# Moving the issue of the padded-key transfers from SyncE to ScalarE in a fused cross-attention and mixture kernel

## The chip, the cores and the metric

The kernel runs on one core of one Trainium2 chip. The metric is the device time of one execution in microseconds. Engines are named as in the profile: PE is TensorE, DVE VectorE, ACT ScalarE, POOL GpSimd, SP SyncE; a q behind the name is that engine's sequencer, which also issues its DMAs.

## The reference, cut to what matters

Sixteen batches of 128 tokens with 256 channels; 32 heads of 8 channels; a mixture of 32 experts follows the attention.

```python
q = (layernorm(x) @ Wq).reshape(b, n, 32, 8)
k, v = split(ctx @ Wkv, 2)                 # ctx: 16 x 128 x 128
q, k = apply_axial_rope(q, pos), apply_axial_rope(k, pos)
w = softmax(einsum('bqhd,bkhd->bhqk', q, k) / sqrt(8))
x = x + einsum('bhqk,bkhd->bqhd', w, v).reshape(b, n, 256) @ Wout + bout
x = x + mixture(layernorm(x))              # gate, top 6 of 32 experts, shared expert
```

## The kernel before, in words

The attention is a software pipeline over batches. Each engine has its own program, a list of periods (`periods`, line 341): periods -3 to 1 and 12 to 17 are written out, 2 to 11 are a hardware loop of five passes with two periods each, so that every even period from 4 on follows a back edge. In period b the engines work on batches b-2 to b+4 at different stages. A period has eight steps g = 0 to 7, one for each quad (4 heads).

For a batch, TensorE computes logits twice. `logits_q` (line 851) has queries on the partitions: four heads at once, from the stationary `qst` and the moving `kz`. `kz` is the padded form of the keys: [128, 4, 8, 128], in which the 32 rows of head j stand in plane j and all else is zero, so that one matmul of 512 columns keeps four heads apart. VectorE takes the row maxima (`row_max`, line 662), TensorE turns them (`transpose_max`, line 855), VectorE copies them to `mxs` (line 669), and SyncE moves them by a DMA of 2 KB into spare rows of `qst` (line 443), two quads at a time: four "halves" a batch, numbered 0 to 3 by `half`. Then `logits_k` (line 864) computes logits again with keys on the partitions, now less their maxima, ScalarE takes the exponential (line 558), and `weigh_values` (line 875) multiplies with V. In period b, steps 0 to 7 of `logits_k` belong to batch b. `logits_q` runs ahead: quads 5 to 7 of batch b in steps 0 to 2, then quads 0 to 4 of batch b+1 in steps 3 to 7. The first of these (step 3) is the first reader of batch b+1's padded keys, and waits for `kz_in`. Maxima halves 2 and 3 of batch b are sent in steps 1 and 3, halves 0 and 1 of batch b+1 in steps 5 and 7. `logits_k` waits for a half at every even step; at step 4 it is half 2, sent in step 1.

How `kz` is filled: the keys of batch b+1 are turned by TensorE (`transpose_k`, line 834) in step 6 of period b-1 and copied by VectorE to `kT` (`evac_kT`, line 697), which signals `kT_ok`. SyncE then issues four DMAs (line 436), one for each group of 32 partitions, 64 KB each, from `kT` into `kz[m1.par]`. There are two `kz` buffers; this one was last read for batch b-1. In SyncE's program the four stand at the top of period b, behind the maxima's transfer of step 7 of the period before, and wait until all exponentials of batch b-1 are done (`exp_ok`), which also implies that `logits_k` of b-1 has finished. In periods -1 and 0 they wait for `kz_zero` and `kT_ok`. Behind them on SyncE come the maxima half 2 (step 1), the context of batch b+4 (line 448), and maxima halves 3, 0 and 1. VectorE's next `evac_kT` waits until the four transfers have read `kT`.

ScalarE's period b (line 552): step 0 is the exponential of quad 0, the copy of V of batch b+1 (line 563), the copy `xcT` of batch b+3 (line 544) and `evac_OT` of batch b-1 (line 608); step 1 an exponential and the copy of `qst` (line 579); step 2 an exponential and the copy of q and k (line 569), which GpSimd's `rope` waits for; step 4 an exponential and `norm`; step 5 the copy `attnT`. In the loop, it also issues the mixture's weight loads, 352 KB each, behind its work of steps 1, 4 and 6 (`load_first`, lines 131 and 133). They are read only in the mixture, from about 292 us. The exponential of quad 0 needs a free `pw` buffer, that is TensorE's `weigh_values` of quad 4 of batch b-1, which stands behind `project_v` (line 841) in TensorE's step 0. The copy of V waits until `weigh_values` of batch b-1 is through. In TensorE's program `transpose_q` (line 827, step 1) waits for this copy, `project_k` (line 816, step 1) for `xcT`, `project_q` (line 820) follows in step 2.

Nothing of the mixture is touched by the change.

Of the kernel before, what the change touches and what calls it, by code (L numbers as in the profile page):

```python
# [36 lines left out]
QUADS, SLOT = NH // 4, 32  # L37
# [237 lines left out]
def attention(nc, sem, X, identf, st2, ring, ahead, hidden, bank, x, ctx_in, pos, wq, wkv, wout, bout):  # L275
    with ExitStack() as es:
# [16 lines left out]
        kT = sb("kT", [P, QUADS, P], F16)  # L293
        kz = [hidden.kz[:, i] for i in range(2)]
# [27 lines left out]
        consts, consts2, kz_zero = sem("consts"), sem("consts2"), sem("kz_zero")  # L322
# [7 lines left out]
        qstT_mm, kstT_mm, qst_ok, kT_ok = sem("qstT_mm"), sem("kstT_mm"), sem("qst_ok"), sem("kT_ok")  # L330
# [10 lines left out]
        def periods(eng, period):  # L341
# [8 lines left out]
            for n in range(12, NB + 2):  # L350
                period(Batch(n // 2, n % 2))

        def inside(b, lo=0, hi=NB - 1):

            return not isinstance(b.n, int) or lo <= b.n <= hi
# [54 lines left out]
        @block.sync  # L410
        def _(sp):
            sp.dma_start(POS[:, :, :], pos.rearrange("b p a -> p b a")).then_inc(pos_in, 16)
            for c in range(4):
                part = slice(XPART[c], XPART[c + 1])
                sp.dma_start(X[:, part, :], xr[:, part, :]).then_inc(x_in[c], 16)
                if c == 0:
                    sp.dma_start(CT[0][:, :], ctx_in[0]).then_inc(ctx_in_s[0], 16)
                    sp.dma_start(WKV[:, 0:D], wkv[:, 0:D]).then_inc(w_in, 16)
                    sp.dma_start(WQ[:, :, :], wq.rearrange("(c p) n -> p c n", p=P)).then_inc(w_in, 16)
                    sp.dma_start(CT[1][:, :], ctx_in[1]).then_inc(ctx_in_s[1], 16)  # L420
            sp.dma_start(WKV[:, D:], wkv[:, D:]).then_inc(bo_in, 16)
            sp.dma_start(BO[:, :], bout.rearrange("(a n) -> a n", a=1).broadcast_to([P, D])).then_inc(bo_in, 16)
            sp.dma_start(WO[:, :, :], wout.rearrange("(c p) n -> p c n", p=P)).then_inc(bo_in, 16)

            def period(b):
                m1, m4 = b + 1, b + 4
                if inside(m1):


                    if isinstance(b.n, int) and b.n < 1:  # L430
                        sp.wait_ge(kz_zero, 2)
                        sp.wait_ge(kT_ok, m1.n + 1)
                    else:
                        sp.wait_ge(exp_ok, QUADS * b.n)
                    for j in range(4):
                        sp.dma_start(kz[m1.par][32 * j:32 * j + 32, j, :, :],
                                     kT[32 * j:32 * j + 32, :, :]).then_inc(kz_in[m1.par], 16)
                for g in (1, 3, 5, 7):
                    who, half = (b, (g + 3) // 2) if g < 5 else (m1, (g - 5) // 2)
                    if inside(who):  # L440
                        k = 4 * who.n + half
                        sp.wait_ge(mxs_ok, k + 1)
                        sp.dma_start(qst[who.par][MAXROW:P:SLOT, 2 * half:2 * half + 2, :],
                                     mxs[half % 2][:, :]).then_inc(mr_in[half % 2], 16)
                    if g == 1 and inside(m4, 2):
                        at_least(sp, xcT_mm, m4.n - 1)
                        sp.wait_ge(consts, 2)
                        sp.dma_start(CT[m4.par][:, :], ctx_in[m4.n]).then_inc(ctx_in_s[m4.par], 16)
            periods(sp, period)
            hidden.store(sp)  # L450

# [78 lines left out]
        @block.scalar  # L530
        def _(act):
            act.wait_ge(turn_s, 5)
            act.activation(ang[:, :, :, :, :], turns[:, :, :, :, :], ACT.Sin, scale=TWO_PI).then_inc(sin_s, 1)

            def norm(m):
                act.wait_ge(rs1_ok, 8 if not isinstance(m.n, int) or m.n > 9 else 6 if m.n > 3 else 4 if m.n else 2)
                at_least(act, xcT_mm, m.n)
                act.activation(xn[:, :], X[:, m.n, :], ACT.Identity, bias=nb1[:, m.n, :],
                               scale=rs1[:, m.n, :]).then_inc(xn_ok, 1)

            def evac_xcT(m):
                at_least(act, xcT_mm, m.n + 1)
                at_least(act, v_mm, m.n - 1)
                act.copy(xcT[m.par][:, :, :], M1[:, 0:3 * P].rearrange("p (c t) -> p c t", c=3)).then_inc(xcT_ok, 1)

            norm(Batch(0, 0))

            def hi(m):
                act.wait_ge(hT_mm, m + 1)
                act.copy(hidden.hT[m // 8][:, 0, :, m % 8 * P:m % 8 * P + P], HBANK[m % 2][:, 0:D].rearrange("p (c t) -> p c t", c=DK)).then_inc(hT_hi, 1)  # L550

            def period(b):
                m1, m2, m3, m4, o = b + 1, b + 2, b + 3, b + 4, b + -1
                for g in range(QUADS):
                    if inside(b):
                        act.wait_ge(st_mm, QUADS * b.n + g + 1)
                        at_least(act, pv_mm, QUADS * b.n + g - 3)
                        act.activation(pw[g % 4][:, :], STB[g % 2][:, :], ACT.Exp, scale=SCALE).then_inc(exp_ok, 1)  # L558
                    if g == 0 and inside(m1):
                        at_least(act, v_mm, m1.n + 1)  # L560
                        act.wait_ge(consts, 7)
                        at_least(act, pv_mm, QUADS * b.n)
                        act.copy(Vh[m1.par][:, :, :, 0:HD], M0[:, 0:D].rearrange("p (f h d) -> p f h d", f=2, d=HD)).then_inc(v_ok, 1)
                    if g == 0 and inside(m3):
                        evac_xcT(m3)
                    if g == 2 and inside(m3) and not (isinstance(b.n, int) and b.n == -3):
                        at_least(act, qk_mm, m3.n + 1)
                        at_least(act, rope_ok, m3.n)
                        act.copy(qk[:, :], M1[:, :]).then_inc(qk_ok, 1)  # L569
                    if g == 5 and inside(o):  # L570
                        act.wait_ge(attnT_mm, o.n + 1)
                        at_least(act, wo_mm, o.n)
                        act.copy(attnT[:, :, :], OB[o.par][:, D:2 * D].rearrange("p (c t) -> p c t", c=DK)).then_inc(attnT_ok, 1)
                    if g == 0 and inside(o):
                        evac_OT(o)
                    if g == 1 and inside(m1):
                            at_least(act, qstT_mm, m1.n + 1)
                            at_least(act, st_mm, QUADS * b.n)
                            act.copy(qst[m1.par][:, :, :], M0[:, :].bitcast(F16).rearrange("p (q t) -> p q t", q=QUADS)).then_inc(qst_ok, 1)  # L579
                    if g == 4 and inside(m4):  # L580
                        norm(m4)

                    if g in (1, 4, 6) and not isinstance(b.n, int):
                        ring.load_first(act, b.n - 2, (1, 4, 6).index(g))
                    if g in (3, 6) and isinstance(b.n, int) and 12 <= b.n < 12 + ahead.PARTS // 2:
                        ahead.load(act, 2 * (b.n - 12) + g // 6, raw_wsg)
                    if g == 7 and isinstance(b.n, int) and b.n == 14:
                        ahead.split_hi(act, raw_wsg)
                    if g > 1 and at(b, NB - 1):
                        hi(g - 2)  # L590
                    if g == 0 and at(b, NB):
                        hi(6)
                        hi(7)
                        act.wait_ge(gwT_mm, 1)
                        act.activation(gwT[:, 0], LT[:, 0:DK * NE].rearrange("p (c e) -> p c e", c=DK), ACT.Copy, scale=WUP).then_inc(gwT_hi, 1)
                        hi(8)
                    if g == 3 and at(b, NB):
                        hi(9)
                    if g == 5 and at(b, NB):
                        hi(10)  # L600
                    if g == 0 and at(b, NB + 1):
                        for m in range(11, NB):
                            hi(m)

            def evac_OT(m):
                act.wait_ge(pv_mm, QUADS * m.n + QUADS)
                at_least(act, ob_mm, m.n)
                act.copy(OT[:, :, :], OB[m.par][:, :].rearrange("p (q t) -> p q t", q=4)).then_inc(OT_ok, 1)
            periods(act, period)


# [955 lines left out]
```

## Time and profile before

| | us |
|---|---|
| median of 3 runs | 358.52 |
| lowest, highest | 358.46, 363.13 |
| the profiled execution | 361.84 |
| its span, first to last instruction | 359.9 |

The attention takes the first 200 us or so of the span. The granted clock of TensorE is 1.00 from 42.7 us to 220 us. The profile is of one execution, so sums made from its rows are differences within that execution; the comparison with the other kernel is made on medians.

In the rows, the first number is the start in microseconds from the span's start, the second the duration; then the engine, the line of the kernel, the operation with output<-input, the shape and the number of instructions merged into one row. In brackets stands the idle time of that engine before it, and who ended it.

### The profile page before, as it was taken

What the parts mean: (1) busy time and instruction counts of PE and PEld (TensorE: products, weight loads), DVE (VectorE), ACT (ScalarE), POOL (GpSimd) and SP (SyncE); (2) the same over time, 40 slices, a digit from 0 to 9 for tenths busy, and PEclk for the clock granted to TensorE, in tenths of its full rate; (3) what the DMA queues carried; (4) which work ended last, traced back from release to release, by engine and by line L of the source; (5) the groups of instructions that cost most, each with busy time, mean ns of one, the idle gap of its engine ahead of it and who ended that gap; (6) DMA issues with size and microseconds to landing.
All of it is one profiled execution on the core that took longest, in us unless ns stands there. A gap on an engine that the chain in (4) does not pass through costs nothing. (4 is left out here: it accounts for less than half of the span.)

```text
span 359.9 us, 9664 instructions
## 1 busy us (share of the span) xinstructions
PE 319.0 (89%) x3152; PEld 223.9 (62%) x3152; DVE 223.3 (62%) x630; ACT 178.7 (50%) x368; POOL 214.0 (59%) x309
## 2 busy tenths in 40 slices
PE   7767899999999999999799788869999989999930
PEld 5536677878778778687567554436675864555520
DVE  3667677766776677776688673784658345455520
ACT  2245567857668676577558621552325343233310
POOL 7697996666876658757459920324698711425460
PEclk9987999999999999999999969989999999999985
DMA  6511105444444454443310410203114365953446
GB/s 159 199 39 39 32 18 140 133 117 127 133 134 122 114 150 117 135 127 96 101 43 8 145 61 29 66 1 87 35 49 141 106 223 181 291 138 41 54 51 233
DMA packets 33437, 37.93 MB, mean 105 GB/s; under 512 B 7824, under 2 KB 27840, under 8 KB 33344
## 3 DMA queue, kind: packets, MB, share of 16 engines
q1 hardware_dynamic: 22754, 22.03, 21.1%
q10 hardware_dynamic: 8030, 11.93, 11.7%
q0 software_dynamic: 2624, 3.61, 6.0%
q8 instruction: 16, 0.26, 0.3%
q14 instruction: 13, 0.11, 0.1%
HBM read 26.36 MB, written 8.96 MB: 98 GB/s over the span
## 5 line engine op out<-in xcount | busy, mean ns | idle before, releaser
L558 ACT ACTIVATE pw<-bank 128x512 f32<-128x512 f32 x128 | 77.6, 611 | 55.9 <-PE bank L875 46.8
L662 DVE TENSOR_REDUCE mx<-bank 128x4 f16<-128x512 f32 x128 | 86.9, 688 | 12.8 <-PE bank L851 11.2
L851 PE MATMUL bank<-kz,qst 128*128 128x512 f16 x128 | 49.4, 387 | 4.7 <-DVE mxs L669 2.2
L864 PE MATMUL bank<-qst,kz 128*128 128x128 f16 x512 | 50.3, 221 | 3.0 <-DMA qst<-mxs 2.9
L864 PEld LDWEIGHTS bank<-qst,kz 128*128 128x128 f16 x512 | 36.5, 99 | 15.5 <-DMA qst<-mxs 4.9
L362 POOL TENSOR_TENSOR work<-work,RC 128x512 f32<-128x512 f32 x15 | 19.1, 1273 | 31.7 <-ACT work L569 31.7
L270 PE MATMUL bank<-kz,WSG 128*128 128x512 f16 (+1 forms) x144 | 33.5, 389 | 3.0 <-ACT ac L1210 2.7
L669 DVE COPY mxs<-bank 8x128 f16<-8x128 f16 x64 | 13.5, 212 | 35.1 <-PE bank L855 35.1
L875 PE MATMUL bank<-pw,V 128*32 128x128 f32 x1024 | 34.6, 276 | 0.0
L875 PEld LDWEIGHTS bank<-pw,V 128*32 128x32 f32 x1024 | 26.0, 109 | 9.1 <-issue 7.4
L1195 POOL DMA_INDIRECT acc<-ac,dst x8 | 11.8, 1475 | 28.6 <-ACT ac L1255 18.2
L270 PEld LDWEIGHTS bank<-kz,WSG 128*128 128x128 f16 (+1 forms) x144 | 15.2, 108 | 19.1 <-ACT ac L1210 3.2
L367 POOL TENSOR_TENSOR work<-work,RS 128x256 f32<-128x256 f32 x30 | 24.8, 849 | 0.0
L387 POOL TENSOR_TENSOR tokst<-work,tokst 128x256 f16<-128x256 f32 x30 | 20.1, 670 | 4.4
L376 POOL TENSOR_TENSOR work<-work 128x256 f32<-128x256 f32 x30 | 21.2, 726 | 2.1 <-POOL work L367 1.7
L1495 PE MATMUL bank<-ring_gu,xbT 128*64 128x352 f32 x112 | 19.1, 461 | 0.8 <-ACT xbT L1104 0.8
L855 PE MATMUL bank<-identh,mx 128*128 128x128 f16 x64 | 14.3, 223 | 4.7 <-DVE mx L662 4.1
L895 PE MATMUL bank<-WO,attnT 128*128 128x256 f32 x64 | 18.3, 411 | 0.0
L851 PEld LDWEIGHTS bank<-kz,qst 128*128 128x128 f16 x128 | 12.5, 98 | 8.3 <-issue 6.0
L1158 POOL TENSOR_TENSOR X<-X,ro 128x256 f32<-128x256 f32 x16 | 14.3, 903 | 4.9 <-ACT ro L1216 4.7
L579 ACT COPY qst<-bank 128x1024 f16<-128x1024 f16 x16 | 16.5, 1032 | 0.8 <-PE bank L827 0.8
L820 PE MATMUL bank<-WQ,xcT 128*128 128x256 f32 x64 | 16.4, 379 | 0.0
(213 smaller groups left out, 667.9 us busy)
## 6 DMA issues: line engine op xcount, KB each, us to landing
ring_gu<-in_L_ffn_w_gate_up ACTq DMA_DIRECT2D x20, 352.0 KB
kz<-kT SPq DMA_DIRECT2D x64, 64.0 KB, 2.0
ring_dn<-in_L_ffn_w_down ACTq DMA_DIRECT2D x10, 352.0 KB
ring_gu<-in_L_ffn_w_gate_up SPq DMA_DIRECT2D x8, 352.0 KB
table<-work SPq DMA_DIRECT2D x8, 256.0 KB, 2.3
acc<-X SPq DMA_DIRECT2D x4, 512.0 KB, 3.1
out<-acc SPq DMA_DIRECT2D x4, 512.0 KB, 5.5
X<-in_x SPq DMA_DIRECT2D x2, 768.0 KB, 8.2
```

What stands on the lines that cost most here:

```text
L270: ins = pe.matmul(GU[2 * (i % 2) + w][0:n, :], ahead.WSG[:, c, u, w * SHARED + a:w * SHARED + a + n], hidden.columns(v, c, 512 * k, 512), ...
L362: eng.tensor_tensor(o1, source[:, :].rearrange("p (x a) -> p x a", a=8), rc, ALU.mult)
L367: ins = eng.tensor_tensor(o2[:, :, :, r], pairs[:, :, :, 1 - r], rs, ALU.mult)
L376: eng.tensor_tensor(rot[:, part], t1[:, part], t2[:, part], ALU.add).then_inc(rot_ok[w], 1)
L387: eng.tensor_tensor(tokst[m.par][:, w, :, a:a + HD], r, hi, ALU.subtract)
L558: act.activation(pw[g % 4][:, :], STB[g % 2][:, :], ACT.Exp, scale=SCALE).then_inc(exp_ok, 1)
L662: dve.tensor_reduce(mx[u // 2 % 2][:, u % 2:8:2], SB[u % 2][:, :].rearrange("p (j t) -> p j t", j=4), axis=AX.X, op=ALU.max, negate=True). ...
L851: pe.matmul(SB[u % 2][:, :], qst[m.par][:, u, :], kz[m.par][:, :, u, :], start=True, stop=True).then_inc(s_mm, 1)
L864: ins = pe.matmul(STB[g % 2][:, j * P:j * P + P], kz[m.par][:, j, g, :], qst[m.par][:, g, :], start=True, stop=True)
L875: ins = pe.matmul(OB[m.par][32 * j:32 * j + 32, (g % 4) * P:(g % 4) * P + P], V[m.par][:, a:a + SLOT], pw[g % 4][:, j * P:j * P + P], star ...
L895: ins = pe.matmul(OB[m.par][:, 0:D], attnT[:, c, :], WO[:, c, :], start=(c == 0), stop=(c == DK - 1))
L1495: ins = pe.matmul(EB[k % 2][lane, 0:2 * INNER], xbT[:, c, e * CAP:e * CAP + LANE], ring.gu[place][:, e % 2, c, :], start=(c == 0), stop=(c ...
```

## The change

From period 1 on (for batches 2 to 15) the four transfers of the padded keys are issued by ScalarE, as the first thing in its period, behind a wait for `kT_ok`. SyncE's wait for `exp_ok` goes, since ScalarE issues them behind its own exponentials of the period before. In periods -1 and 0 SyncE issues them as it did.

```diff
+        def pad_keys(eng, m):
+
+            for j in range(4):
+                eng.dma_start(kz[m.par][32 * j:32 * j + 32, j, :, :], kT[32 * j:32 * j + 32, :, :]).then_inc(kz_in[m.par], 16)
+
...
             def period(b):
                 m1, m4 = b + 1, b + 4
-                if inside(m1):
-
-
-                    if isinstance(b.n, int) and b.n < 1:
-                        sp.wait_ge(kz_zero, 2)
-                        sp.wait_ge(kT_ok, m1.n + 1)
-                    else:
-                        sp.wait_ge(exp_ok, QUADS * b.n)
-                    for j in range(4):
-                        sp.dma_start(kz[m1.par][32 * j:32 * j + 32, j, :, :],
-                                     kT[32 * j:32 * j + 32, :, :]).then_inc(kz_in[m1.par], 16)
+                if inside(m1) and isinstance(b.n, int) and b.n < 1:
+                    sp.wait_ge(kz_zero, 2)
+                    sp.wait_ge(kT_ok, m1.n + 1)
+                    pad_keys(sp, m1)
...
             def period(b):
                 m1, m2, m3, m4, o = b + 1, b + 2, b + 3, b + 4, b + -1
+                if inside(m1) and not (isinstance(b.n, int) and b.n < 1):
+                    act.wait_ge(kT_ok, m1.n + 1)
+                    pad_keys(act, m1)
                 for g in range(QUADS):
```

## Rows read from the trace of the kernel before

**Rows 1.** The page, busy time of TensorE over the span.
```profile
PE 319.0 (89%) x3152; PEld 223.9 (62%) x3152; DVE 223.3 (62%) x630; ACT 178.7 (50%) x368; POOL 214.0 (59%) x309
```
**Rows 2.** Waits from 50 to 176 us: total, times, longest; weight loads, then ScalarE.
```profile
PEld bank L864 <- DMA qst<-mxs: 4.9, 9, 1.0
...
ACT pw L558 <- PE bank L875: 34.2, 23, 2.1
```
**Rows 3.** Timeline, project_v: start of periods 4, 7, 8, 12 and 14.
```profile
73.07 0.59 PE L841 MATMUL bank<-WKV,xcT 128*128 128x256 f32 x2
...
106.89 0.59 PE L841 MATMUL bank<-WKV,xcT 128*128 128x256 f32 x2
...
117.61 0.59 PE L841 MATMUL bank<-WKV,xcT 128*128 128x256 f32 x2
...
161.94 0.59 PE L841 MATMUL bank<-WKV,xcT 128*128 128x256 f32 x2
...
185.40 0.59 PE L841 MATMUL bank<-WKV,xcT 128*128 128x256 f32 x2
```
**Rows 4.** Timeline of period 7, from kT to the fifth group of logits_k.
```profile
105.36 0.68 DVE L697 COPY kT<-bank 128x1024 f16<-128x1024 f16 x1
...
106.63 0.54 SPq L443 DMA_DIRECT2D qst<-mxs  x1
...
107.30 2.46 SPq L436 DMA_DIRECT2D kz<-kT  x4
...
107.91 0.60 ACT L558 ACTIVATE pw<-bank 128x512 f32<-128x512 f32 x1 [1.89 <-PE bank L875]
...
108.64 0.37 ACT L563 COPY V<-bank 128x256 f32<-128x256 f32 x1
...
109.08 0.48 ACT L544 COPY xcT<-bank 128x384 f32<-128x384 f32 x1
...
109.30 0.61 PE L827 MATMUL bank<-identh,tokst 128*128 128x128 f16 x8
...
109.39 0.21 DVE L669 COPY mxs<-bank 8x128 f16<-8x128 f16 x1 [1.16 <-PE bank L855]
...
109.75 0.65 PE L816 MATMUL bank<-WKV,xcT 128*128 128x256 f32 x2
...
109.87 0.58 SPq L443 DMA_DIRECT2D qst<-mxs  x1
...
110.13 0.39 ACTq L131 DMA_DIRECT2D ring_gu<-in_L_ffn_w_gate_up  x1
...
111.31 0.64 ACT L558 ACTIVATE pw<-bank 128x512 f32<-128x512 f32 x1
...
111.80 0.64 ACT L569 COPY work<-bank 128x512 f32<-128x512 f32 x1
...
112.48 0.39 PE L864 MATMUL bank<-qst,kz 128*128 128x128 f16 x4
```
**Rows 5.** Timeline of period 6: maxima's copy, weight load, maxima, TensorE's fifth group.
```profile
97.88 0.21 DVE L669 COPY mxs<-bank 8x128 f16<-8x128 f16 x1 [1.15 <-PE bank L855]
...
98.61 0.39 ACTq L131 DMA_DIRECT2D ring_gu<-in_L_ffn_w_gate_up  x1
98.69 0.59 SPq L443 DMA_DIRECT2D qst<-mxs  x1
...
101.83 0.40 PE L864 MATMUL bank<-qst,kz 128*128 128x128 f16 x4 [0.71 <-DMA qst<-mxs]
```
**Rows 6.** Timeline of period 13: SyncE's key transfers, then their first reader.
```profile
173.37 3.58 SPq L436 DMA_DIRECT2D kz<-kT  x4
...
178.43 0.38 PE L851 MATMUL bank<-kz,qst 128*128 128x512 f16 x1 [0.96 <-issue]
```
**Rows 7.** Timeline, ScalarE: an issue of 32 partitions, and the activation behind it.
```profile
182.84 0.56 ACTq L170 DMA_DIRECT2D gw<-in_L_ffn_gate_w  x1
...
183.50 0.60 ACT L558 ACTIVATE pw<-bank 128x512 f32<-128x512 f32 x1 [0.40 <-PE bank L864]
```

## The prediction

> **What bounds the kernel now.** I read the page first: TensorE is busy for 89% of the span, no other engine for more than 62% [rows 1]. Then the waits between 50 and 176 us, the middle of the attention. TensorE's one wait on another unit that recurs there is for the small transfer of the row maxima, qst<-mxs: 4.9 us in nine waits. The key transfer kz<-kT isn't in that list at all. ScalarE for its part waits 34.2 us in 23 waits for TensorE's products with V, 1.5 us each, before an exponential [rows 2]. So the order of importance is TensorE's own stream, then the maxima, and ScalarE has holes.
>
> Third, the length of a period, taken between the starts of project_v (line 841, once a period), called T0 below. Period 7 runs from 106.89 to 117.61, 10.72 us. Periods 4 to 11 together run from 73.07 to 161.94, 88.87 us [rows 3]; at 10.7 each they would take 85.6, so 3.3 us are lost. The losses sit in the even ones, the first after the loop's back edge: period 6 waits for maxima at 101.83 (0.71 us of TensorE) [rows 5]. Periods 12 and 13 together run from 161.94 to 185.40, 23.46 [rows 3], 2.1 too much.
>
> Fourth, the timeline of one period without a loss (7) and of one with it (6). In period 7 SyncE issues four key transfers in 2.46 us, ending at 109.76. The maxima copy ends at 109.60, so its transfer waits 0.27 for SyncE and goes at 109.87, ahead of ScalarE's weight load of 110.13; TensorE takes the fifth group of keys at 112.48 without a wait [rows 4]. In period 6 the order is turned: the copy ends at 98.09, the weight load goes at 98.61, the maxima only at 98.69, and TensorE gets them at 101.83, 3.1 us later; in period 7 2.6 us had been enough [rows 4, 5]. The maxima lose a race that the four key transfers ahead of them on SyncE made close.
>
> **The change, part by part.** It acts in 14 periods (1 to 14); periods -1 and 0 keep SyncE.
>
> *Taken from SyncE:* four issues, 2.46 us a period, and their wait for the exponentials. The maxima of the second half can now be issued as soon as they are copied: 109.60 in place of 109.87 in period 7 [rows 4], 98.09 in place of 98.69 in period 6 [rows 5], each ahead of the weight load, which moves later if it moves at all. That takes the 3.3 us of periods 4 to 11. In period 13 the four issues took 3.58 us in place of 2.46, and TensorE stood 0.96 us at 178.43, ahead of the product that needs the new keys, and then for the maxima [rows 6]: on ScalarE they start about 1.2 us sooner. I let the 2.1 us of periods 12 and 13 go, 0.5 and 1.6 by my estimate from that stall. Sum of the gains: 5.4 us. The first group after the top is not affected: its maxima are issued before the keys, as before.
>
> *Added to ScalarE:* one wait for kT_ok and four issues, ahead of the exponential of the first quad. kT is complete at 105.36 + 0.68 = 106.04 [rows 4]; 0.05 for the signal. ScalarE's sequencer is free by then, since the last exponential of the period before is dispatched. One issue: the nearest row on ScalarE's own queue is a transfer of 32 partitions, like these, 0.56 us [rows 7]; on SyncE the four took 2.46, 0.615 each [rows 4]. So 2.24 to 2.46 us for four, ending at 108.33 to 108.55. From the end of an issue to the next activation: 182.84 + 0.56 = 183.40, and the activation starts at 183.50, 0.10 [rows 7]. The exponential that started at 107.91 starts at 108.43 to 108.65: of the 2.3 us, 1.8 lie in its old wait, 0.5 to 0.7 stick out.
>
> What is queued behind it: the copy of V, the copy xcT, then OT, the second exponential, the copy of qst. V had slack of its own, for it waited for TensorE's last product with the old V: it started 0.73 after the exponential, while an activation of this size lets the next start after 0.49 (111.31 to 111.80) [rows 4]. So V starts at 108.92 to 109.14 in place of 108.64 and ends 0.37 later; with 0.05 for the signal, transpose_q can start at 109.34 to 109.56 in place of 109.30. xcT follows V without a gap, 0.48, and project_k can start at 109.82 to 110.04 in place of 109.75 [rows 4]. TensorE loses 0.07 to 0.29 us a period. I take 0.2, nearer the upper end, since issues have small gaps between them. 14 x 0.2 = 2.8 us. Further down ScalarE's chain there is more room: the third exponential (111.31 + 0.64, moved by 0.5 at most, 112.45) is what the fifth group of keys at 112.48 needs [rows 4], and TensorE is itself 0.2 late by then.
>
> *Moved past a queue:* the key transfers now lie on ScalarE's queue, behind the third weight load of the period before, and beside the maxima of SyncE. Their data may come later behind that load; but they start 1.2 us sooner than at 107.30 [rows 4], and TensorE doesn't wait for keys in these periods [rows 2]. Cost nil; if that cover failed it would be a wait ahead of the first product of the next batch. ScalarE's own weight loads move by at most 0.7 us and are not read before the mixture. GpSimd waits for ScalarE's copy qk in each period; a delay of 0.5 lies within its idle time.
>
> A rule of the Trainium skill speaks against this part. Two queues do issue at once here: SyncE from 109.87 to 110.45, ScalarE from 110.13 to 110.52, neither longer than its usual 0.58 and 0.39 [rows 4]. Perfetto Trace Analysis, section DMA Instruction — HWDGE, says that an issuing sequencer locks a shared descriptor generator for its exclusive use and that the wait for the lock is in the profiled time. By it the rows above should be longer, so the trace doesn't bear it out for this pair; it is the second rival.
>
> Sum: 2.8 - 5.4 = -2.6 us. The profiled execution took 361.84 us (span 359.9), so 359.2 for a like one; against the median of 358.52 it is 355.9. That execution lies 3.3 above the median, so differences and not its level are carried over.
>
> **Rivals.**
>
> 1. *The hole in ScalarE swallows everything.* If issues are nearer 0.5 us, or kT comes a little sooner, TensorE loses nothing and the gains stand alone: 358.5 - 5.4 = 353.1. For it: ScalarE's wait of 1.89 ahead of that exponential, and V's slack of 0.24 [rows 4]. Against: 2.24 of four issues at the only like row.
>
> 2. *Slower: the two queues block each other.* The maxima of the first half go from SyncE at 106.63 for 0.54 us [rows 4], now in the middle of ScalarE's four issues. If they exclude each other, ScalarE ends 0.54 later, all of it behind the slack: 0.2 + 0.54 = 0.74 a period, 10.4 us in 14, less 5.4: 363.5. It decides against the change from 5.4 / 14 = 0.39 us a period on, that is 0.2 us more than I take, 0.05 an issue. Against it: the overlap in rows 4. For it: that is a single kind of pair, and four issues in a row were not seen on ScalarE.
>
> 3. *The maxima aren't cured.* Their late arrival could be the traffic, not the order: 0.6 us sooner, they still travel among key data and weights. Then only period 13 gains, 1.6 us, and 2.8 are paid: 359.7. For it: 2.6 to 3.1 us from issue to use [rows 4, 5] for 2 KB. DMA: Bandwidth & Descriptors, section Issuing engines are not separate DMA queues, takes this side: a second issuer saves sequencer time alone, since all queues end on the same engines. Against: periods 6 and 7 carry the same loads and differ in order and in half a microsecond only.
>
> 4. *The slow issues move along.* In period 13 four issues took 1.1 us too long [rows 6]; if that belongs to the moment and not to SyncE, ScalarE stands there in place of it. Twice at most (periods 12 and 13), 2.2 us: 358.1.
>
> **How the numbers follow.** Forecast 0.47, rival 1 0.15, rival 2 0.16, rival 3 0.14, rival 4 0.08. The predicted time is 355.9, a gain of 0.7%. The range goes from rival 1, with half a microsecond for the wait for keys that period 14 may lose too, to just under rival 2: 352.6 to 363.0. About 2% is what a measurement of this kernel can tell from no change, 7.2 us, so 351.3 and 365.7. No case reaches the lower; it is left 0.05. The upper needs rival 2 with a lock longer than one issue: 0.08. Within: 0.87.
>
> **What would show it.** Right: in the loop kz<-kT appears on ScalarE's queue from about 0.8 us before T0, 0.56 to 0.62 each; the first exponential starts 1.5 to 1.8 after T0 (now 1.02), and the one wait ahead of it is gone; transpose_q waits 0.04 to 0.3 for V; SyncE's second-half maxima go 2.8 after T0; even and odd periods are equal, near 10.9; TensorE's waits for qst<-mxs in 50 to 176 us vanish. Wrong: periods of 11.2 or more with issues of 0.7 us and up on either queue (rival 2); waits for maxima still in even periods (rival 3); one issue of over 1 us on ScalarE near 163 or 174 us (rival 4); a new wait ahead of the first product with the new keys, which I have at nil.

## The result, and the profile after

The changed kernel takes 367.06 us (median of 4 runs, 365.09 to 367.85) against 360.82 us for the kernel before on the same chips. The ratio is 1.019, interval 1.013 to 1.025: slower, though the interval leaves open whether by 2%, where a gain of 0.7% was forecast, to 355.9 us and at the most 363.0. Its profiled execution took 365.09 us, its span is 363.0. The runs of the kernel before reach from 358.46 to 363.92, so medians decide only about sizes of one per cent; what moves inside is read from the length of single periods. Each kernel has one trace; in that of the kernel before, the odd periods of the loop lie between 10.63 and 10.72 us.

From the changed kernel's page, a group of its fifth part (busy time, mean of one in ns | idle time before it, and who ended it) and, from the sixth, its key transfers (us to landing last):

```profile
L828 PE MATMUL bank<-identh,tokst 128*128 128x128 f16 x128 | 9.7, 218 | 9.8 <-ACT V L564 9.8
...
kz<-kT ACTq DMA_DIRECT2D x56, 64.0 KB, 2.8
```

The first line is most of the story. TensorE's transpose_q (now line 828) stood 9.8 us waiting for ScalarE's copy of V; in the kernel before, that wait isn't in the list at all. The waits for the maxima shrank. The same list as [rows 2], from 50 to 176 us:

```profile
ACT pw L559 <- PE bank L876: 36.7, 21, 3.0
...
PEld bank L828 <- POOL tokst L394: 7.7, 10, 0.8
PE bank L828 <- ACT V L564: 6.0, 11, 1.3
...
PEld bank L865 <- DMA qst<-mxs: 1.8, 6, 0.5
```

4.9 us became 1.8 for the maxima; 6.0 us of V are new. The nine waits of the kernel before were of two kinds: four in the even periods at the fifth group of keys, 3.3 us, which are gone, and five ahead of the first group of the next batch, 1.6 us, of which kind all six are that are left, 1.8 us. The line on GpSimd's copy tokst belongs to the same stand, for `transpose_q` needs both tokst and V; in each period of the loop tokst was done 0.4 to 0.6 us ahead of V (in period 7 at 110.92 against 111.35), so V ended the wait. Timeline of period 7 of the changed kernel (T0, the start of project_v, is 108.38), to be laid beside [rows 4]:

```profile
106.85 0.68 DVE L698 COPY kT<-bank 128x1024 f16<-128x1024 f16 x1
...
107.56 2.72 ACTq L356 DMA_DIRECT2D kz<-kT  x4
...
110.49 0.60 ACT L559 ACTIVATE pw<-bank 128x512 f32<-128x512 f32 x1 [2.99 <-PE bank L876]
...
110.98 0.37 ACT L564 COPY V<-bank 128x256 f32<-128x256 f32 x1
...
111.12 0.54 SPq L441 DMA_DIRECT2D qst<-mxs  x1
...
111.49 0.61 PE L828 MATMUL bank<-identh,tokst 128*128 128x128 f16 x8 [0.54 <-ACT V L564]
...
112.33 0.40 ACTq L131 DMA_DIRECT2D ring_gu<-in_L_ffn_w_gate_up  x1
```

The bracket at 110.49 needs care: it puts 2.99 us of ScalarE's idle time down to TensorE's product, but that had long been done. ScalarE wasn't waiting; its sequencer was issuing DMAs from 107.56 to 110.28, which isn't counted as busy. Relative to T0, the exponential moved from 1.02 to 2.11, V from 1.75 to 2.60, transpose_q from 2.41 to 3.11. The maxima went at 2.74 and not at 2.98, ahead of the weight load, as forecast; and the weight load, which ScalarE issues behind its own work, went at 3.95 in place of 3.24.

Lengths of the periods, each from one start of project_v to the next (the line of [rows 3]):

| period | 1 | 2 | 3 | 4 | 5 | 6 | 7 | 8 | 9 | 10 | 11 | 12 | 13 | sum |
|---|---|---|---|---|---|---|---|---|---|---|---|---|---|---|
| before | 10.63 | 10.67 | 10.63 | 11.60 | 10.70 | 11.52 | 10.72 | 11.42 | 10.63 | 11.56 | 10.72 | 11.19 | 12.27 | 144.3 |
| after | 12.13 | 11.45 | 11.33 | 11.31 | 11.35 | 11.30 | 11.37 | 11.57 | 11.04 | 11.42 | 11.30 | 12.62 | 13.56 | 151.8 |

Even and odd periods are now alike, as forecast, but at 11.35 and not at 10.9. Periods 1, 12 and 13 are longer still. In each of them one of the four issues is very long; the 2.1 us that the kernel before lost in periods 12 and 13 weren't won, and the two together went from 23.46 to 26.18 us. For the changed kernel, the key issues from 39 to 43 us (duration in ns: least, median, most), from 163.5 to 168 and from 176 to 180:

```profile
L356 ACTq DMA_DIRECT2D kz<-kT x4: 597/606/1352, 39.1 to 41.7; - x4
...
L356 ACTq DMA_DIRECT2D kz<-kT x4: 514/602/1573, 164.2 to 166.3; - x4
...
L356 ACTq DMA_DIRECT2D kz<-kT x4: 545/731/1405, 176.8 to 178.9; - x4
```

Period 13 has one more loss, of the clock. The table by stage (length, busy time of PE, PEld, DVE, ACT, POOL, granted clock, DMA share and GB/s) for period 7, for the long wait, for the two microseconds behind it, and for what followed:

```profile
108.38:119.75 11.37, 10.83 (x147) 8.46 (x146) 7.87 (x18) 7.55 (x15) 7.69 (x13) 1.00 0.50 123
176.80:181.40 4.60, 3.11 (x49) 1.93 (x47) 3.07 (x7) 0.98 (x3) 2.56 (x7) 1.00 0.43 122
...
181.40:183.40 2.00, 1.44 (x19) 1.11 (x20) 0.69 (x1) 2.00 (x4) 0.00 (x0) 1.00 0.00 0
...
183.30:186.70 3.40, 3.40 (x35) 2.55 (x39) 2.29 (x5) 1.23 (x3) 0.00 (x0) 0.52 0.29 78
```

TensorE had been busy 3.11 of 4.60 us and then 1.44 of 2.00; from 183.4 to 186.8 the clock was then granted at 0.50, its level of 1.2 GHz. What brought it down isn't shown: a wait of 1.33 us in period 1 of this trace, and one of 1.64 in period 1 of the kernel below with a loop of four passes, were followed by no fall.

The two profiled executions differ by 3.1 us in span and not by the 7.5 of the table, and outside the table it is the clock in which they differ. The kernel before had its clock at 0.50 in three stretches outside the periods of the table: from 24.6 to 31.4, from 208.9 to 215.7 and from 239.6 to 243.0 us (so it was not at 1.00 up to 220 us, as was said ahead of the prediction). The changed kernel's trace has none there, though in these parts the change touches only period 14's four issues: it starts period 1 at 39.51 and not at 41.14, and from the start of period 14 to the end it takes 171.7 us and not 174.5. That the clock makes these 1.6 and 2.8 us is argued, not shown. In all twelve traces this last part lies between 171.6 and 175.4 us.

### The profile page after: what moved, and what is told of

Its sections match the earlier page's. It is cut to its first block and busy times, and to the rows that moved or that the text cites. A ratio compares the mean times of both kernels' runs of the same rounds, so it can differ in the third digit from the quotient of the medians.

```text
span 363.0 us, 9654 instructions
## 1 busy us (share of the span) xinstructions
PE 314.5 (87%) x3152; PEld 220.1 (61%) x3152; DVE 224.7 (62%) x630; ACT 176.0 (48%) x368; POOL 214.7 (59%) x309
## 5 line engine op out<-in xcount | busy, mean ns | idle before, releaser
L559 ACT ACTIVATE pw<-bank 128x512 f32<-128x512 f32 x128 | 78.6, 619 | 68.2 <-PE bank L876 44.3
L270 PE MATMUL bank<-kz,WSG 128*128 128x512 f16 (+1 forms) x144 | 32.2, 379 | 3.0 <-ACT ac L1211 2.7
L828 PE MATMUL bank<-identh,tokst 128*128 128x128 f16 x128 | 9.7, 218 | 9.8 <-ACT V L564 9.8
L896 PE MATMUL bank<-WO,attnT 128*128 128x256 f32 x64 | 17.4, 394 | 0.1
```

Source lines behind the costliest of these rows:

```text
L270: ins = pe.matmul(GU[2 * (i % 2) + w][0:n, :], ahead.WSG[:, c, u, w * SHARED + a:w * SHARED + a + n], hidden.columns(v, c, 512 * k, 512), ...
```

## The experiments

My theory after the result, A: ScalarE's sequencer is held by the issues, and what passes its old first exponential, less V's slack, goes to TensorE. Its rival, B: a second queue beside SyncE's, or behind the weight loads, costs in itself. For the old loss in even periods there was also a question left: do the maxima come late by SyncE's order, or by traffic?

**Two and two.** Edit of the changed kernel:

```diff
+                elif inside(m1):
+                    sp.wait_ge(exp_ok, QUADS * b.n)
+                    pad_keys(sp, m1, (2, 3))
...
-                    pad_keys(act, m1)
+                    pad_keys(act, m1, (0, 1))
```

> From period 1 on ScalarE issues the transfers of heads 0 and 1, SyncE those of heads 2 and 3 at its old place. Theory A (the cost is the time that ScalarE's sequencer is held, as far as it passes the start of its old first exponential): two issues end about 0.4 us after the start of project_v, the exponential starts at 1.02 as before, all periods 4 to 11 are 10.7 us, and the time is 4 to 5 us under the kernel before, ratio 0.987. Theory B (the cost is that two queues issue or carry side by side): both queues are used at once even longer than in the changed kernel, single issues last 0.7 us or more, periods stay at 11.2 or more, ratio at least 1.01.

356.12 us, ratio to the kernel before 0.990 (0.987 to 0.994). The first exponential is at 1.01 to 1.02 in the loop, and transpose_q at 2.42; all thirteen periods lie between 10.5 and 11.0, the sum of periods 1 to 13 is 139.6. In the loop, issues on both queues at once last no longer than alone; around 73 us:

```profile
L356 ACTq DMA_DIRECT2D kz<-kT x2: 529/573/617, 72.5 to 73.1; - x2
L356 SPq DMA_DIRECT2D kz<-kT x1: 577/577/577, 74.6 to 74.6; - x1
...
L444 SPq DMA_DIRECT2D qst<-mxs x1: 527/527/527, 73.1 to 73.1; - x1
```

ScalarE's second issue started at 73.09 and the maxima's on SyncE at 73.10. The one departure is period 1, where SyncE's two took 0.69, beside ScalarE's second, and 0.76 us, alone. A holds, B doesn't: half of the change is a gain.

**One ahead, all on SyncE.** Edit of the kernel before. The first key transfer of the next period goes ahead of the maxima of step 7, three stay behind. VectorE's copy kT also waits for the batch's last logits, so that kT_ok says that the buffer is free:

```diff
-                    for j in range(4):
+                    for j in range(0 if isinstance(b.n, int) and b.n < 1 else 1, 4):
...
+                        m2 = b + 2
+                        if g == 7 and inside(m2) and not (isinstance(b.n, int) and b.n < 0):
+                            sp.wait_ge(kT_ok, m2.n + 1)
+                            sp.dma_start(kz[m2.par][0:32, 0, :, :], kT[0:32, :, :]).then_inc(kz_in[m2.par], 16)
...
+                o = m + -2
+                if inside(o):
+                    dve.wait_ge(st_mm, QUADS * o.n + QUADS)
```

> All four key transfers on SyncE, but the first goes ahead of the maxima's transfer of step 7, three behind it; VectorE's copy kT waits for the last logits of the batch, some 0.05 us. Order theory (even periods lost 0.8 us because SyncE was late with the maxima of step 1): the maxima of step 1 go at 2.8 us after project_v in all periods, even ones fall from 11.5 to 10.7, 3 us gained, ratio 0.991. Traffic theory (the maxima are late because of data on the same engines): no gain, ratio 0.998 to 1.003, even periods stay at 11.5.

353.99 us, ratio 0.986 (0.978 to 0.993), the lowest median of the study (of four runs), and better than both kernels. The periods sum to 139.7; periods 4, 6, 8 and 10 are 10.75, 10.64, 10.91 and 10.64. Period 6, T0 at 94.41:

```profile
93.01 0.69 DVE L704 COPY kT<-bank 128x1024 f16<-128x1024 f16 x1
...
93.73 0.56 SPq L445 DMA_DIRECT2D kz<-kT  x1
...
94.40 0.53 SPq L447 DMA_DIRECT2D qst<-mxs  x1
...
95.43 1.84 SPq L436 DMA_DIRECT2D kz<-kT  x3
...
96.92 0.21 DVE L673 COPY mxs<-bank 8x128 f16<-8x128 f16 x1 [1.08 <-PE bank L862]
...
97.41 0.59 SPq L447 DMA_DIRECT2D qst<-mxs  x1
...
97.65 0.39 ACTq L131 DMA_DIRECT2D ring_gu<-in_L_ffn_w_gate_up  x1
```

The hole that was used lay ahead of the maxima of step 7: kT is ready at 93.70, the maxima only at 94.1. The maxima of step 1 go at 3.00 after T0 (0.32 sooner than in [rows 5]), 0.24 ahead of the weight load, and the wait is gone. The loop of the kernel before shows the same by itself: its even periods from 4 on send these maxima at 3.30 to 3.44 and the weight load at 3.23 or 3.24, and wait; in period 2 and in the odd ones the maxima go at 2.75 to 3.09, ahead of the load, and nobody waits for them. Ahead of that lies when SyncE starts on the keys: 0.70 to 0.83 after T0 in those even periods, 0.17 to 0.41 in the odd ones; why the back edge makes this difference wasn't tried.

**A pause on ScalarE.** The kernel before, with keys on SyncE, and at the top of periods 1 to 13 on ScalarE six copies that nobody needs:

```diff
+                    act.wait_ge(kT_ok, m1.n + 1)
+                    flat = ahead.WSG[:, :, :, :].rearrange("p c a f -> p (c a f)")
+                    for n in range(6):
+                        w = 512 if n < 5 else 256
+                        act.activation(flat[:, 512 * n:512 * n + w], WKV[:, 0:w], ACT.Copy)
```

> The kernel before (keys on SyncE), with a pause on ScalarE at the top of periods 1 to 13: a wait for kT_ok and five and a half needless copies, some 2.8 us, as long as the four issues. Theory A: the pause alone makes the whole cost: exponential at about 2.0 after project_v, transpose_q late by 0.6, odd periods 11.3; even periods the same, since the late maxima are hidden by the pause; ratio 1.02 as with the change. Theory B: with no second queue in use the cost is not there or is small, odd periods under 10.9, ratio under 1.01.

364.07 us, ratio 1.015 (1.007 to 1.023). In the loop, but for period 4, the exponential is at 1.9 to 2.1 and transpose_q at 2.8 to 3.1, as in the changed kernel, though no key transfer had moved to another queue. Its list of waits from 39 to 192 us:

```profile
PE bank L836 <- ACT V L572: 6.1, 12, 0.9
...
PE bank L873 <- DMA qst<-mxs: 1.4, 1, 1.4
```

The loop's periods are 11.1 to 11.5, apart from periods 3 and 4 (12.79 and 10.64) around that one wait of 1.4. Periods 6, 8 and 10 are 11.37, 11.43 and 11.45: with SyncE's order as it was and a pause added, they are as long as in the kernel before (11.52, 11.42, 11.56). So the pause costs nothing in them, and what the change "gained" in even periods it would have had from a pause of this size on ScalarE. Why, a part of period 6 shows (T0 at 97.18):

```profile
100.56 0.59 SPq L443 DMA_DIRECT2D qst<-mxs  x1
...
101.08 0.40 ACTq L131 DMA_DIRECT2D ring_gu<-in_L_ffn_w_gate_up  x1
...
103.43 0.39 PE L873 MATMUL bank<-qst,kz 128*128 128x128 f16 x4
```

The maxima go at 3.38, as late as in the kernel before, but the pause holds ScalarE's weight load back too, to 3.90, so they are ahead of it again. TensorE also comes for them 0.66 later; how much of the relief is due to which isn't separated here, but a run below takes the load away alone. The pause makes more than half of the cost (the sum of the periods is 148.4, of which 0.8 or so go to the one wait, against 144.3 and 151.8); what the change costs beyond it sits in periods 1, 12 and 13, where this kernel has 11.67, 11.38 and 11.41 against 12.13, 12.62 and 13.56, for here the long issues stay on SyncE.

**One issue for 256 KB, on SyncE and on ScalarE.** Edits of the kernel before and of the changed kernel, from period 1 on, with the semaphore's counts to match. Both leave out the padded form, for all keys go to plane 0; their logits are not those of the reference, and only their times are used:

```diff
-                    for j in range(4):
-                        sp.dma_start(kz[m1.par][32 * j:32 * j + 32, j, :, :],
-                                     kT[32 * j:32 * j + 32, :, :]).then_inc(kz_in[m1.par], 16)
+                        sp.dma_start(kz[m1.par][:, 0, :, :], kT[:, :, :]).then_inc(kz_in[m1.par], 16)
...
-                    pad_keys(act, m1)
+                    act.dma_start(kz[m1.par][:, 0, :, :], kT[:, :, :]).then_inc(kz_in[m1.par], 16)
```

> The kernel before, but from period 1 on one transfer of 128 partitions with the same 256 KB in place of four of 32 (the keys all go to plane 0, so the padded form isn't made and the logits differ). It is the relief of SyncE by itself, nothing on ScalarE. Order theory: maxima of step 1 go at once, all periods 10.7, periods 12 and 13 too, 5 us gained, ratio 0.986. Traffic theory: the bytes are the same, even periods stay at 11.5, ratio above 0.995.

> The changed kernel, but from period 1 on ScalarE issues one transfer of 128 partitions with the same 256 KB in place of four (all keys to plane 0, so the logits differ). The bytes travel on ScalarE's queue, behind the third weight load, as in the change; only the time that its sequencer is held is gone. Theory A (held time): exponential at 1.02, all periods 10.7, no long waits, ratio 0.985, as with one issue on SyncE. Theory B (the queue behind the weight load, or two queues side by side, costs): periods 11 and more, a wait for kz ahead of the first product with the new keys, ratio 1.00 or more.

354.6 us, ratio 0.985 (0.976 to 0.995), and 356.3 us, ratio 0.985 (0.978 to 0.992). The periods sum to 139.3 and 139.1, even ones at 10.6 to 10.9 in both. On ScalarE's queue the bytes need 3.8 us from issue to landing against 2.3 on SyncE's:

```profile
kz<-kT SPq DMA_DIRECT2D x14, 256.0 KB, 2.3
```

```profile
kz<-kT ACTq DMA_DIRECT2D x14, 256.0 KB, 3.8
```

Nobody waits for these 1.5 us. The bytes are the same and lie behind the same weight loads, so bytes and queue are free here; what costs is the number of issues and whom they hold.

**Three and one.** As two and two, with `(0, 1, 2)` on ScalarE and `(3,)` on SyncE.

> From period 1 on ScalarE issues three of the four, SyncE the last one. Theory A with its slack: three issues end at 1.3 after project_v, with 0.18 to the exponential 1.45, V at 1.94 in place of 1.75, transpose_q at 2.45 in place of 2.41: next to nothing, periods 10.7 to 10.75, ratio 0.99; the fourth issue alone makes the cost. If the cost is in proportion to the issues instead, transpose_q is late by three quarters of 0.68, periods 11.2, ratio 1.012.

358.47 us, ratio 0.990 (0.986 to 0.994). Period 7, T0 at 107.29:

```profile
108.76 0.60 ACT L562 ACTIVATE pw<-bank 128x512 f32<-128x512 f32 x1 [2.34 <-PE bank L879]
...
109.25 0.37 ACT L567 COPY V<-bank 128x256 f32<-128x256 f32 x1
...
109.77 0.61 PE L831 MATMUL bank<-identh,tokst 128*128 128x128 f16 x8
```

The exponential is at 1.47, V at 1.96, transpose_q at 2.48, 0.07 late. The first three issues cost 0.07 us, the fourth 0.63 more: the slack is real, and it ends at about three. Only period 1, with its long issue, still lost 1.1.

**The weight load of step 6 issued earlier.** Edit of the changed kernel: steps `(1, 4, 6)` of the three loads become `(1, 2, 4)`, so two of the loads move.

> The changed kernel with the weight loads of steps 1, 4, 6 issued in steps 1, 2, 4. If the third key issue lasts 0.88 us, and not 0.61, because the weight load of step 6 still fills ScalarE's queue, then it falls to 0.61, the four take 2.45 in place of 2.72, transpose_q starts at 2.8 in place of 3.1, periods 11.1 in place of 11.35, 2.5 us less than the changed kernel: ratio to the kernel before 1.011. If that length belongs to the issue itself or to SyncE's issue beside it, nothing moves: 0.88, 11.35, ratio 1.018.

373.58 us, ratio 1.032 (1.027 to 1.037): both expectations missed. The third issue stays at 0.87 to 0.89 us, so the weight load ahead of it isn't its cause. The periods in the loop are 11.6 to 12.3, for a reason that I hadn't foreseen. Its waits from 39 to 192 us, and its timeline in period 6 (T0 at 103.46):

```profile
PE bank L865 <- DMA qst<-mxs: 8.2, 18, 0.8
...
PE bank L828 <- ACT V L564: 3.9, 5, 1.7
```

```profile
108.73 0.39 ACTq L131 DMA_DIRECT2D ring_gu<-in_L_ffn_w_gate_up  x1
...
108.99 0.55 SPq L441 DMA_DIRECT2D qst<-mxs  x1
...
112.06 0.38 PE L865 MATMUL bank<-qst,kz 128*128 128x128 f16 x4 [0.42 <-DMA qst<-mxs]
```

The maxima of step 3 now go 0.26 us behind the load of step 2 and TensorE gets them 3.1 us after their issue: the very loss of the even periods, in another step and in eight of the ten loop periods. The other ten of the 18 waits are ahead of the first group of the next batch. Its maxima go 0.9 us behind the load of step 4, as they do in the changed kernel, but here with the load of step 2 two microseconds ahead of that one: in period 6 they go at 111.58 and TensorE gets them at 115.11, 3.5 us later. Both spoke for the loads as the cause, which the next run was made for.

**No weight load in step 1.** Edit of the kernel before; the ten loads are issued by SyncE after the attention:

```diff
-                    if g in (1, 4, 6) and not isinstance(b.n, int):
+                    if g in (4, 6) and not isinstance(b.n, int):
...
             hidden.store(sp)
+            for k in range(RESIDENT):
+                ring.load_first(sp, k, 0)
```

> The kernel before without ScalarE's weight load of step 1 in the loop; those ten loads are issued by SyncE after the attention. SyncE's order and times around the maxima stay as they were (even periods: maxima of step 1 at 3.3 to 3.4 after project_v). Race theory (in even periods the maxima fall in behind that weight load): even periods fall from 11.5 to 10.7 to 10.8, and TensorE's waits for the maxima at the fifth group go. Lateness theory (0.35 us later is too late by itself): even periods stay at 11.4 or more. The mixture may pay for the moved loads, so this is read from the periods.

358.38 us, ratio 0.996 (0.992 to 1.000). SyncE is as late as before; period 6, T0 at 95.20:

```profile
94.93 0.53 SPq L443 DMA_DIRECT2D qst<-mxs  x1
...
95.96 2.47 SPq L436 DMA_DIRECT2D kz<-kT  x4
...
97.71 0.21 DVE L671 COPY mxs<-bank 8x128 f16<-8x128 f16 x1 [1.09 <-PE bank L857]
...
98.57 0.59 SPq L443 DMA_DIRECT2D qst<-mxs  x1
...
100.79 0.39 PE L866 MATMUL bank<-qst,kz 128*128 128x128 f16 x4
```

The maxima go at 3.37 after T0, 0.65 behind their copy, and still periods 4, 6, 8 and 10 fall to 10.71, 10.70, 10.98 and 10.77. TensorE takes them without a wait 2.2 us after their issue, against 2.9 to 3.1 behind the load. Lateness alone costs next to nothing; lateness past the weight load costs 0.8 us. Order and traffic aren't rivals: the order decides whether the traffic is ahead. The periods sum to 140.6, 3.7 less than before; that the median gains less wasn't followed up.

**Loop of four passes.** The changed kernel with periods 10 and 11 written out.

> The changed kernel with periods 2 to 9 in the hardware loop (four passes) and 10, 11 written out. Of ScalarE's key issues one each in periods 1, 12 and 13 lasts 1.35 to 1.57 us, and within 1 us of each of these a 16 KB packet of queue 8 (instructions) passes. Code theory: the long issues go with the fetching of written-out code, so one moves to period 10 or 11, and 12 or 13 loses one; periods with a long issue are longer by 0.8. Place theory: they belong to periods 12 and 13 whatever the code: both keep theirs, 10 and 11 get none.

One run, 365.01 us, too few for its time to be compared. The key issues of periods 10 and 12:

```profile
141.76 3.11 ACTq L356 DMA_DIRECT2D kz<-kT  x4
...
164.93 2.72 ACTq L356 DMA_DIRECT2D kz<-kT  x4
```

The long issues left periods 12 and 13, whose issues now take the loop's 2.72, and a longer one came into period 10 (its fourth takes 0.99 us against 0.61) and into period 11 (3.05 us for the four). The DMA view has a 16 KB packet of the instruction queue in 143 to 144 and 155 to 156 us here, at just these issues, and in 40 to 41, 166 to 167 and 178 to 179 us in the changed kernel. The first of these packets (queue and kind: packets, MB, share of 16 engines):

```profile
q8 instruction: 1, 0.02, 5.8%
```

So long issues go with the fetching of written-out code, though the two new ones are shorter (0.3 to 0.4 us over, not 0.7 to 1.0). The other traces bear it out: in the ten with four key issues a period, 26 of these issues last over 0.9 us, on SyncE as on ScalarE, all in written-out periods, and each starts within 0.8 us of the start of such a packet. Which written-out period gets one differs from kernel to kernel (the kernel of three and one has its long ones in periods 1 and 14), so that periods 12 and 13 lost theirs here says little by itself. That a fetch holds an issue is shown only by this coincidence; how it does so wasn't tried.

**One on ScalarE, one ahead and two behind on SyncE.** The second experiment's kernel, with the fourth transfer given to ScalarE:

```diff
-                    for j in range(0 if isinstance(b.n, int) and b.n < 1 else 1, 4):
+                    for j in (range(4) if isinstance(b.n, int) and b.n < 1 else (1, 2)):
...
+                    act.wait_ge(kT_ok, m1.n + 1)
+                    act.dma_start(kz[m1.par][96:128, 3, :, :], kT[96:128, :, :]).then_inc(kz_in[m1.par], 16)
```

> The kernel of e2 (one key transfer on SyncE ahead of the maxima of step 7), of the other three two behind it on SyncE and one on ScalarE at the top of its period. By theory A one issue on ScalarE is free (it ends before its old first exponential), and SyncE is done 0.6 us sooner than in e2: periods 10.65, the long periods 12 and 13 at 11.0 or less, 0.5 to 1 us under e2, ratio 0.984. If a second queue costs anything in itself, it is at or above e2's 0.986 to 0.99.

356.33 us, ratio 0.990 (0.986 to 0.994) where 0.984 was expected, the periods sum to 139.5. By the ratio alone this is where the expectation put rival B; the issues themselves speak against it. In period 4 the two queues' key issues start together and last as long as alone:

```profile
73.24 0.57 SPq L445 DMA_DIRECT2D kz<-kT  x1
73.24 0.53 ACTq L560 DMA_DIRECT2D kz<-kT  x1
```

Periods 12 and 13 are 10.71 and 10.48, as expected, but period 3 is 11.30, with a wait of 0.5 us for maxima. The sum is that of the second experiment to 0.2 us: the last issue on SyncE wasn't in anyone's way any more. Whether this one or the one with all four on SyncE is the better can't be told from these intervals.

## Why the prediction was wrong

Right by its steps: SyncE's relief. The maxima went at once, even and odd periods became equal, and the 3.3 us of waits at the fifth group went. The gain that I put at 5.4 us is 5.0 where nothing is paid for it (144.3 to 139.3 us with one issue on SyncE). That all waits for maxima would vanish was too much: the waits ahead of a batch's first group, which the prediction itself called unaffected, stayed at 1.8 us. Also right were the start of the issues (kT's end plus 0.03), the path V, transpose_q, project_k, and that the place of the bytes costs nothing. The lock between two queues (rival 2) isn't seen in any loop period; what could be read so is period 1 of the kernels of two and two and of three and one, where an issue of SyncE beside one of ScalarE's took 0.69 and 0.70 us.

Wrong was the cost on ScalarE, the step *Added to ScalarE*: 0.2 us a period, 2.8 in all, where 0.70 was measured in period 7 and 10.8 over periods 1 to 13. The term was mis-sized in each of its parts, all to the same side. Against my middle, four issues took 2.72 us and not 2.35: the first 0.53, then 0.61, 0.88 and 0.61, with gaps between them. The hand-over to the exponential took 0.2 in the loop and not 0.10; [rows 7] come from period 13, and in the written-out periods 1, 12, 13 and 14 of the changed kernel it is indeed 0.10. Transpose_q's weight load started 0.11 after V's end and its first product 0.14 after it, not 0.05, a term for which I had no row. Together 0.70 in place of 0.2. My own break-even was 0.39 a period; the estimate lay 0.2 under it, made of a single issue of 0.56 and of rows of the other queue. The right reading of so thin a margin would have been that its sign is open. Thirteen waits make 8.9 us in the list up to 192 us; transpose_q's start, against 2.41 in the kernel before (2.26 in period 13), is late by 10.8 us in these thirteen periods, for before the change it began some 0.2 us under the end of the product ahead of it, which a wait takes away as well.

Rival 4, at 0.08, came true beside it, and with it the 2.1 us that I let go in periods 12 and 13 weren't won: the long issues came along, and the written-out period 1 got one too. They cost 0.8 us each in periods 1 and 12 and 0.6 in 13, where transpose_q is at 3.91, 3.91 and 3.72. The clock's 3.4 us at 1.2 GHz add up to 1.7 in period 13, by my estimate from the half rate; the prediction had no term for it. Check of the sum: 139.3 without losses, 10.8 for V, the long issues in it, and 1.7 for the clock are 151.8, and 151.8 were measured. That it closes so well is partly luck: in period 12 alone transpose_q is 1.5 late and the period 1.9 longer than with one issue on SyncE.

One step of the reasoning, not of size: gains and costs were added, as if independent. They aren't. Holding ScalarE at the top of its period also pushes its weight load of step 1 back (3.24 to 3.9) and lets TensorE come later for the maxima, and the run with the pause shows even periods that pay nothing for late maxima with SyncE's order unchanged. This kernel thus had either loss, not both, and moving the issues exchanged one, in every second period, for one in all.

## What to carry to other kernels

An issue held the sequencer that made it, here ScalarE's for 2.72 us a period. Before moving issues to a compute engine, lay their full length (with the hand-over behind them) beside the hole in that engine's timeline, and move only so many as fit; and read them from rows of the same code, loop or written out. Here two or three of four were free and the fourth turned a gain of 1% into a loss of 2%. A small transfer that someone waited for had to be issued ahead of the bulk load of another queue, and another order on the same queue did that as well as any second queue.

## What the runs showed that I had not expected

The third of four successive issues on ScalarE lasted 0.86 to 0.89 us against 0.61 for the second and fourth, in all loop periods of the changed kernel, with and without a weight load in step 6 and with the fourth issue on SyncE, and 0.62 in period 14. Its cause stays open. A 2 KB transfer issued 0.06 to 0.35 us behind a 352 KB load of another queue was there 2.9 to 3.3 us after its issue; without that load it was there within 2.2. And a wait's bracket named TensorE for 2.99 us in which ScalarE's own sequencer was issuing: idle time of an engine that issues DMAs has to be read together with its queue's rows.
